# Where polynomials, a last squaring and layer-norm roots stand in a vision transformer's one-core program

## The reference

```python
h = tokens + positions                               # [32, 38, 256]
h = h + attention(layernorm(h))                      # 16 heads of 16, q and k layer-normalized, causal
h1 = h;  z = layernorm(h1)                           # then the FFN's own layernorm with gamma, beta
abel = gelu(xn @ abel_w + abel_b)
logits = xn @ moe_gate_w + moe_gate_b                # 8 experts, top 2, softmax of the two
moe = sum_e w_e * (gelu(xn @ ew1[e] + eb1[e]) @ ew2[e] + eb2[e])
for i in range(3): moe = moe @ expm(gens[i])         # 256 x 256 skew matrices
gate = sigmoid(concat(abel, moe) @ gc_w + gc_b)
out = h1 + residual + abel * (1 - gate) + moe * gate # residual: the FFN's input
```

## Time and profile before

| | |
|---|---|
| three runs | 383.19, 384.49, 385.95 us; median 384.49 |
| the profiled execution | 384.6 us, its span 382.7 us |
| busy, share of the span | TensorE 332.1 us (87%), VectorE 223.6 (58%), ScalarE 175.5 (46%), GpSimd 152.8 (40%) |
| mean granted TensorE clock | 0.955 |
| chain that ended last, by engine | TensorE 71%, VectorE 13%, issue 7%, DMA 4%, ScalarE 2% |
| stages, from the start of the span | attention 75 to 165 us, projection to 188, router and powers to 211, slots to 346, last stage to 380 |

### The profile page before, as it was taken

The page is one execution under the profiler, slowest core; times in us unless marked ns, Lnnn a source line. Parts: engine busy times, 40 slices in busy tenths (PEclk is TensorE's granted clock), DMA queues, the critical chain, the costliest instruction groups (busy, mean ns, idle before and its releaser), DMA issues.

```text
span 382.7 us, 6792 instructions
## 1 busy us (share of the span) xinstructions
PE 332.1 (87%) x2010; PEld 280.3 (73%) x2010; DVE 223.6 (58%) x598; ACT 175.5 (46%) x417; POOL 152.8 (40%) x168
## 2 busy tenths in 40 slices
PE   2999799949999999949989796999999998993895
PEld 1787354539888888836777685999899997892894
DVE  0235459787989999886887287795313231010175
ACT  1000254378898989514433662434344444450231
POOL 1002804050456546361022217588534667852000
PEclk9999899976999999978998999999999999998599
DMA  8742511124111110076404353455324555551442
GB/s 260 269 134 64 200 57 54 55 78 136 48 48 48 46 46 6 2 305 229 143 8 139 97 149 87 149 153 161 115 85 151 167 165 166 178 152 60 144 142 90
DMA packets 20544, 45.78 MB, mean 120 GB/s; under 512 B 2150, under 2 KB 12836, under 8 KB 20260
## 3 DMA queue, kind: packets, MB, share of 16 engines
q1 hardware_dynamic: 17732, 37.80, 30.4%
q0 software_dynamic: 2496, 6.82, 5.3%
q10 hardware_dynamic: 288, 0.81, 0.8%
HBM read 38.20 MB, written 7.22 MB: 119 GB/s over the span
## 4 chain that ended last, share of the span: by engine, by line
PE 71%; DVE 13%; issue 7%; DMA 4%; ACT 2%; POOL 1%; DVEq 1%; POOLq 0%; ACTq 0%; SPq 0%
PE banks L1447 10%; PE banks L1456 9%; PE banks L1389 8%; PE banks L1232 5%; PE banks L1202 5%; PE banks L1309 5%; PE banks L1285 4%; PE banks L1522 3%; PE banks L1327 3%; PE banks L1360 3%; PE banks L1532 3%; PE banks L1272 2%; PE banks L1218 2%; PE banks L1237 2%; PE banks L1258 2%
## 5 line engine op out<-in xcount | busy, mean ns | idle before, releaser
L1447 PE MATMUL banks<-qn_sb,w_sb 128*128 128x128 f32 x416 | 50.9, 275 | 1.0 <-ACT qn_sb L628 1.0
L1456 PE MATMUL banks<-w_sb,sq_sb 128*128 x208 | 49.2, 380 | 0.8 <-DVE pT_sb L1124 0.7
L1447 PEld LDWEIGHTS banks<-qn_sb,w_sb 128*128 128x128 f32 x416 | 48.6, 192 | 1.2 <-ACT qn_sb L628 1.2
L628 ACT ACTIVATE qn_sb<-banks,col_sb 128x128 f32<-128x128 f32 x52 | 21.1, 457 | 56.9 <-PE banks L1434 55.0
L456 POOL DMA_INDIRECT y_rows<-pT_sb,sidx_sb x26 | 25.9, 998 | 45.5 <-DVE pT_sb L1124 43.1
L1456 PEld LDWEIGHTS banks<-w_sb,sq_sb 128*128 128x128 f32 x208 | 38.4, 190 | 6.0 <-issue 1.4
L639 ACT ACTIVATE sq_sb<-banks,col_sb 128x128 f32<-128x128 f32 x104 | 32.4, 369 | 14.8 <-PE banks L1447 13.3
L1124 DVE TENSOR_TENSOR pT_sb<-banks,p_sb 128x256 f32<-128x256 f32 x26 | 11.0, 424 | 47.5 <-PE banks L1456 25.3
L1202 PE MATMUL banks<-wtok_sb,patch_sb 128*114 128x256 f32 x132 | 30.4, 393 | 7.8 <-DMA wtok_sb<-in_w_tok 7.6
L450 POOL DMA_INDIRECT qn_sb<-z_rows,gidx_sb x26 | 28.7, 1103 | 20.1 <-PE banks L1434 13.2
L1202 PEld LDWEIGHTS banks<-wtok_sb,patch_sb 128*114 128x114 f32 x132 | 24.3, 186 | 13.4 <-DMA patch_sb<-in_patches 7.5
(11 more groups left out here) (221 smaller groups left out, 653.2 us busy)
## 6 DMA issues: line engine op xcount, KB each, us to landing
w_sb<-in_w SPq DMA_DIRECT2D x26, 512.0 KB
w_sb<-in_w SPq DMA_DIRECT2D x1, 4096.0 KB, 12.6
patch_sb<-in_patches SPq DMA_DIRECT2D x11, 342.0 KB, 3.1
vrep_sb<-v_rows SPq DMA_DIRECT2D x33, 114.0 KB
qk_sb<-y_rows SPq DMA_DIRECT2D x10, 228.0 KB
v_rows<-v_sb SPq DMA_DIRECT2D x11, 114.0 KB
z_rows<-h_sb SPq DMA_DIRECT2D x11, 114.0 KB
out_rows<-h_sb SPq DMA_DIRECT2D x10, 114.0 KB
```

The costliest lines, as they stand in the source:

```text
L1447: last = nc.tensor.matmul(bank[2 + 2 * s + c // 2][:, (c % 2) * 128:(c % 2 + 1) * 128], w1_sb[:, w0:w0 + 128], xsT_sb[:, (2 * s + k) * 128 ...
L1456: last = nc.tensor.matmul(bank[6 + s][:, 0:D], hidT_sb[:, s * HID + k * 128:s * HID + (k + 1) * 128], w2_sb[:, ds(e * 4 * D + k * D, D)], ...
```

## The change

- `P0_AT` and `P1_AT` go from 2 and 5 to 3 and 6. VectorE runs `poly_first(j)` behind `slot_step(j)` for j = 0, 1, 2, where 0 and 1 stood ahead of slot 0 and 2 behind it.
- Only two of the last three squarings stay in slots 10 and 11. The third matrix is transposed in slot 19 (`LAST_AT`), its product follows behind the last slot. The chain's second product also follows there, in bank 4; its transpose is made in slot 20. `third()` runs behind VectorE's last slot and does two of its steps before the product.
- The roots come in three batches cut at `CUT = (7, 10)`: tiles 0 to 6, whose variances are set in step 8 and whose power stands ahead of `gather_images(9)`; 7 to 9; and 10. `norm_z(0)` and `norm_z(1)` stand ahead of VectorE's `select(10)`, the others are reordered, and `top(t-2)` follows `keep_pre(t)`.
- The ten sizing operations move to the attention's start (`size_generators`), the two scalings to ScalarE, in steps 8 and 9.
- One-column activations on a zero draw the Exp table behind `root(1)`, the Gelu table ahead of the slots, and the Exp table again behind the last Gelu.
- `turn_att(10)`, `output(10)` and `keep_attT(10)` stand one tile later; `rank()` behind the first product, `invert()` behind the seventh.

```diff
@@ -269,8 +269,10 @@
         EARLY = 4
-        P0_AT, P1_AT, MORE_AT, SQ_AT, E_AT = 2, 5, 9, 10, (14, 16)
+        P0_AT, P1_AT, MORE_AT, SQ_AT, E_AT = 3, 6, 9, 10, (14, NS)
         MORE_BANK = (0, 4, 5)
+        LAST_AT = 19
+        CUT = (7, 10)
@@ -428,15 +430,17 @@
             for t in range(NT):
+                if t == NT - 1:
+                    powers(1, 0, CUT[0])
...
                     spread(t + 1)
-            powers(1, 0, 8)
             gather_images(NT - 1)
-            powers(2, 8, NT)
+            powers(2, CUT[0], CUT[1])
+            powers(3, CUT[1], NT)
@@ -524,6 +528,7 @@
             root(1)
+            nc.scalar.activation(al_sb[:, 78:79], con_sb[:, K_ZERO:K_ZERO + 1], ACT.Exp)
@@ -578,6 +583,14 @@
                     keep_attT(t - 1)
+                if isinstance(t, int) and t in (8, 9):
+                    scale_generators(t - 8)
+
+            def scale_generators(n):
+                act.wait_ge(d_gen, 32)
+                act.wait_ge(scale_set, 1)
+                m = (a_sb, aT_sb[:, :])[n]
+                nc.scalar.activation(m, m, ACT.Copy, scale=nrm_sb[:, 12:13]).then_inc(n_scaled, 1)
@@ -597,7 +610,7 @@
             for t in range(NT):
-                if t == 3:
+                if t == 4:
@@ -649,6 +662,11 @@
+            def keep_ET(n, k):
+                act.wait_ge(e_turned, n + 1)
+                nc.scalar.activation(YT[k], bank[0][:, :], ACT.Copy).then_inc(e_evac, 1)
+
+            nc.scalar.activation(al_sb[:, 79:80], con_sb[:, K_ZERO:K_ZERO + 1], ACT.Gelu)
@@ -656,12 +674,14 @@
                 u = j - SQ_AT
-                if 0 <= u < G:
-                    keep_YT(3 * more + u + 1, u % G, 0)
-                if j in E_AT:
-                    n = E_AT.index(j)
-                    act.wait_ge(e_turned, n + 1)
-                    nc.scalar.activation(YT[n], bank[0][:, :], ACT.Copy).then_inc(e_evac, 1)
+                if 0 <= u < 2:
+                    keep_YT(3 * more + u + 1, u, 0)
+                if j == E_AT[0]:
+                    keep_ET(0, 0)
+                if j == LAST_AT:
+                    keep_YT(3 * more + 3, 2, 0)
+                if j == LAST_AT + 1:
+                    keep_ET(1, 1)
@@ -686,6 +706,7 @@
+            nc.scalar.activation(al_sb[:, 77:78], con_sb[:, K_ZERO:K_ZERO + 1], ACT.Exp).then_inc(exp_warm, 1)
@@ -883,11 +904,13 @@
                     norm_k(t + 3, 1 - s)
+                if isinstance(t, int) and t == NT - 1:
+                    norm_z(0)
+                    norm_z(1)
                 select(t, s)
-                if isinstance(t, int) and t == 9:
-                    aggregate(mv2_sb, 0, 8, NT, h1_stats)
-                    variances(0, 8)
-                    scale_generators()
+                if isinstance(t, int) and t == 8:
+                    aggregate(mv2_sb, 0, CUT[0], NT, h1_stats)
+                    variances(0, CUT[0])
@@ -898,8 +921,7 @@
-            def scale_generators():
-                dve.wait_ge(d_gen, 32)
+            def size_generators():
@@ -911,9 +933,13 @@
                 link(nc.vector.tensor_tensor(nrm_sb[:, 11:12], nrm_sb[:, 10:11], nrm_sb[:, 10:11], ALU.subtract))
-                link(nc.vector.tensor_tensor(nrm_sb[:, 12:13], nrm_sb[:, 9:10], nrm_sb[:, 11:12], ALU.add))
-                for m in (a_sb, aT_sb[:, :]):
-                    nc.vector.tensor_scalar(m, m, nrm_sb[:, 12:13], None, ALU.mult).then_inc(n_scaled, 1)
+                nc.vector.tensor_tensor(nrm_sb[:, 12:13], nrm_sb[:, 9:10], nrm_sb[:, 11:12], ALU.add).then_inc(scale_set, 1)
+
+            def norm_z(t):
+                if t in (0,) + CUT:
+                    dve.wait_ge(rstd2, 1 if t == 0 else 2 + CUT.index(t))
+                nc.vector.tensor_scalar(h_sb[0:T, t * D:(t + 1) * D], h1_sb[0:T, t * D:(t + 1) * D], mv2_sb[0:T, 2 * t:2 * t + 1],
+                                        R[1][:, t:t + 1], ALU.subtract, ALU.mult).then_inc(zrow_set, 1)
@@ -921,17 +947,12 @@
             shift(0, 0)
+            size_generators()
...
             idx3 = idx_sb[0:T, :].rearrange("p (t k) -> p t k", k=8)
-
-            def norm_z(t):
-                if t in (0, 8):
-                    dve.wait_ge(rstd2, 1 + t // 8)
-                nc.vector.tensor_scalar(h_sb[0:T, t * D:(t + 1) * D], h1_sb[0:T, t * D:(t + 1) * D], mv2_sb[0:T, 2 * t:2 * t + 1],
-                                        R[1][:, t:t + 1], ALU.subtract, ALU.mult).then_inc(zrow_set, 1)
@@ -945,24 +966,25 @@
-            for t in range(3):
+            for t in range(2, 5):
...
             finish(NT - 2)
-            norm_z(3)
+            aggregate(mv2_sb, CUT[0], CUT[1], NT, h1_stats)
+            variances(*CUT)
             keep_pre(0)
-            norm_z(4)
+            norm_z(5)
             keep_pre(1)
+            norm_z(6)
             finish(NT - 1)
-            aggregate(mv2_sb, 8, NT, NT, h1_stats)
-            variances(8, NT)
+            aggregate(mv2_sb, CUT[1], NT, NT, h1_stats)
+            variances(CUT[1], NT)
             for t in range(2, NT):
-                if t + 3 < NT:
-                    norm_z(t + 3)
                 keep_pre(t)
-                if t >= 4:
-                    top(t - 4)
-            for t in range(NT - 4, NT):
-                top(t)
+                if t + 5 < NT:
+                    norm_z(t + 5)
+                top(t - 2)
+            top(NT - 2)
+            top(NT - 1)
@@ -1133,35 +1155,31 @@
             def third():
+                link(nc.vector.tensor_tensor(Y[0], Y[0], Y[2], ALU.add))
+                for m in range(2):
+                    diagonal = Y[0][:, m * D + m * 128:m * D + m * 128 + 128]
+                    link(nc.vector.tensor_tensor(diagonal, diagonal, eye, ALU.add))
                 dve.wait_ge(e_made, 2)
-                link(nc.vector.tensor_tensor(Y[0], Y[0], Y[2], ALU.add))
                 link(nc.vector.tensor_tensor(yw3[:, :, 0:D], Y[0].rearrange("p (k d) -> p k d", k=2),
-                                             bank[0][:, :].rearrange("p (k d) -> p k d", k=2), ALU.add))
-                for k in range(2):
-                    diagonal = yw3[:, k, k * 128:(k + 1) * 128]
-                    link(nc.vector.tensor_tensor(diagonal, diagonal, eye, ALU.add))
+                                             bank[4][:, :].rearrange("p (k d) -> p k d", k=2), ALU.add))
...
-            poly_first(0)
-            poly_first(1)
...
                 u = j - SQ_AT
-                if 0 <= u < G:
-                    square(3 * more + u + 1, u % G, 0)
+                if 0 <= u < 2:
+                    square(3 * more + u + 1, u, 0)
...
                     second()
-                if j == E_AT[1]:
-                    third()
                 slot_step(j, j % 2, j // 2 if j >= 2 else None)
-                if j == 0:
-                    poly_first(2)
+                if j < G:
+                    poly_first(j)
@@ -1171,7 +1189,9 @@
                             square(3 * i + n + 1, n, MORE_BANK[n])
-
+            square(3 * more + 3, 2, 0)
+            dve.wait_ge(s_kept_cr, 3 * more + G + 3)
+            third()
@@ -1363,14 +1383,14 @@
             for t in range(NT):
-                if t == 3:
-                    turn_att(NT - 1, 0, False)
...
                     output(NT - 2, False)
+                if t == 3:
+                    turn_att(NT - 1, 0, False)
...
                     pre(t - 1, (t - 1) % 2)
-                if t == 3:
+                if t == 4:
@@ -1414,9 +1434,9 @@
                 product(bank[6 + k % 2], AT[n], (A, A2, A3)[k // G][n]).then_inc(x_made, 1)
-                if k == 1:
+                if k == 0:
                     rank()
-                if k == 5:
+                if k == 6:
@@ -1468,14 +1488,17 @@
                                      stop=True).then_inc(counted, 1)
-                if 0 <= u < G:
+                if 0 <= u < 2:
                     pe.wait_ge(s_kept_cr, 3 * more + G + u)
-                    turn_square(bank[0], Y[u % G]).then_inc(s_turned, 1)
-                if j in E_AT:
-                    if j == E_AT[0]:
-                        pe.wait_ge(s_kept_cr, 3 * more + 2 * G)
-                    else:
-                        pe.wait_ge(e_kept, 1)
+                    turn_square(bank[0], Y[u]).then_inc(s_turned, 1)
+                if j == E_AT[0]:
+                    pe.wait_ge(s_kept_cr, 3 * more + G + 2)
+                    turn_square(bank[0], Y[0]).then_inc(e_turned, 1)
+                if j == LAST_AT:
+                    pe.wait_ge(e_kept, 1)
+                    turn_square(bank[0], Y[2]).then_inc(s_turned, 1)
+                if j == LAST_AT + 1:
+                    pe.wait_ge(s_evac, 3 * more + 3)
@@ -1489,13 +1512,12 @@
                     product(bank[0], A4T[n], poly[n]).then_inc(p_made, 1)
-                if 0 <= u < G:
+                if 0 <= u < 2:
                     pe.wait_ge(s_evac, 3 * more + u + 1)
-                    product(bank[0], YT[u % G], Y[u % G]).then_inc(s_made, 1)
```

(13 more changed lines are left out.)

6 lines of the change are left out of this document (3 added, 3 removed).

## The result

The changed kernel takes 370.65 us (median of four runs: 368.37, 368.76, 372.54, 372.73), the kernel before beside it 384.58: a ratio of 0.9632, 95% interval 0.9573 to 0.9692. Its profiled execution took 372.73 us (span 370.9, mean granted clock 0.972), one of the two longer ones; against the 384.6 us of the profile before that is 11.9 us, while the medians are 13.9 apart. I forecast 367.5 us, range 363.5 to 374.5.

The account below looks back on a forecast made before the run. TensorE was busy 87% of the span, with holes at the attention's start and end, the slots' start and before the last stage. 4.4 + 1.8 + 1.7 + 5.8 + 3.4 = 17.1 us; 384.6 - 17.1 = 367.5, range 363.5 to 374.5.

Parts of the forecast that it names:

- Attention's start: Sizing operations and early Exp draw at the attention's start cost and gain nothing: 0, bounds 0 and 1.5 us lost.
- Attention's end: First transpose of normalized rows starts earlier, half clock gone, VectorE newly waits for output(10): gain 4.4 us, bounds 1.5 to 6.5.
- rival (c): output(10) and VectorE's queue hold the attention's end, router's half clock returns: 1.5 instead of 6.2, 372.2 us; chance 0.19.
- Router: Fewer tops, moved rank and inversion, half clock gone in three products, Gelu draw before slots: gain 1.8 us, bounds -1 and 3.5.
- Slots' start: Slot 0's result no longer follows two polynomials, 3.74 us hole goes, slot 4 waits 3.3: gain 1.7 us, bounds 0 and 5.0.
- a longer one kept 1.00: Slot 4's wait: the trace was taken to show full clock after a longer gap, against the skill's warning.
- rival (d): The wait in slot 4 drops the clock, half clock behind it: 369.8 to 370.9 us; chance 0.06.
- Slots' end: Two products leave slots 12 and 16 (3.5 us), third() leaves slot 16 (2.3): gain 5.8 us, bounds 3.5 and 5.9.
- None over 0.5 us behind slot 16: Sign for the late slots: no TensorE wait over 0.5 us behind slot 16.
- Last stage: Moved products shrink TensorE's idleness from 7.6 to 3.3 us, half clock at stage's start goes: gain 3.4 us, bounds -1 and 3.4.
- so I take the whole: Last stage: clock stayed full over a 3.74 us hole, so the whole 3.4 us half-clock loss counts as gained.
- Rival (b): The clock falls over the last wait after all: 1.1 instead of 3.4, 369.8 us, up to 372; chance 0.24.

Follow-up runs that it names:

- f0: The changed kernel again with no edit, beside new runs of the kernel before: 369.67 us, ratio 0.9662.
- g3: The changed kernel without the three early draws of tables on ScalarE: 370.91 us, ratio 0.9635.
- f3: The changed kernel with rank() back behind the second product and invert() behind the sixth: 369.53 us, ratio 0.9644.
- e4: The changed kernel with six more matmuls into an unread bank, keeping TensorE busy before the last stage: 370.58 us, ratio 0.9669.
- f2: The changed kernel with six more matmuls into an unread bank in slot 4, ahead of the wait for poly_second(0): 373.82 us, ratio 0.9742.
- e3: The changed kernel with the attention's end as before (sizing, scaling, roots, normalized rows), rank() and invert() kept at new places: 378.2 us, ratio 0.9886.

## Why the prediction was right, and where not

The forecast, 367.5, is 3.1 us below the median; the direction and most mechanisms held, two on the clock did not, and some of the agreement is luck (below). By its own terms (forecast; in the first profile after; in f0's):

- **Attention's start**, 0: right. TensorE's waits before `turn_q(1)` and `turn_k(1)` are only divided otherwise: 1.94 and 3.44 us before, 3.45 and 1.92 now. From the attention's first transposes to P10 it takes 85.51 us before and 85.47 now, so the sizing, the draw and the first scaling cost nothing; g3 shows it for the draw alone.
- **Attention's end**, 4.4; 4.2; 4.2. The steps held: scalings of 1.57 us (1.5), power 2.65 (2.9), VectorE's wait 2.27 before `finish(10)` (1.8). That the sum is so close is luck, since two sizes were off and cancel: the first transpose came 4.6 us behind P10 where I had 5.3, and from there the last `pre` took 18.05 us where I had 17.1. So that stretch is no shorter than the 17.91 of before although its half clock is gone, and this much of rival (c) came true; its price did not.
- **Router**, 1.8; 2.2; 2.0. The wait before `rank()` is 1.20 us (1.1), and no half clock behind the inversion. But I gave the half clock to the waits that the new places remove; f3 has those waits and no fall, so this 1.9 of the 2.5 us has no shown cause and may be the one execution's. The Gelu load costs nothing, since gather 0's landing comes last there.
- **Slots' start**, 1.7; 0.5; 0.5. Steps and sizes held: hole gone, `poly_second(0)` from 227.3 to 230.4, a wait of 2.61 (3.3). The failed step is the clock behind that wait, of which I wrote "a longer one kept 1.00": rival (d), which I gave 0.06, came true in every profile with this wait, 3.4 us of half clock, so 1.7 us lost. Without it this part would be 2.2, by estimate.
- **Slots' end**, 5.8; 4.0; 5.4. The two products' 3.5 us are sure. The rest depends on gathers: 0.58 us and smaller waits in the first profile, none over 0.25 in f0. "None over 0.5 us behind slot 16" was too strong.
- **Last stage**, 3.4; -0.4; 1.2 (last projection to end: 38.62, 38.98, 37.45). The step that failed, "so I take the whole", failed twice: the clock was not kept, and the clock is not worth that much there. TensorE's idleness shrank as worked out (7.55 to 2.95 us), but the single hole of 3.74 us over which the clock had stayed was the exception: behind idleness of 2.59 us or more it fell in every later case. And 6.8 us at half clock cost TensorE 3.4 us but the stage 1.7 (27.91 against e4's 26.22), because with a fast TensorE the stores' transfers end it. Rival (b) had the mechanism right, and its 1.1 us is f0's figure.
- **Not in the sum**: 1.3 us (f0: 2.5) from the stretch up to P10. Of these 1.3 (f0: 2.0) lie ahead of the attention's first transposes, where nothing is changed; the profile before had half clock from 41.2 to 44.6 us there and those two had none. This is luck of the executions.

So 4.2 + 2.2 + 0.5 + 4.0 - 0.4 + 1.3 = 11.8 us of span for the first profile, 4.2 + 2.0 + 0.5 + 5.4 + 1.2 + 2.5 = 15.8 for f0's (both with rounding; 11.8 and 15.7 measured). Without the start, the change's own gains are 10.5 and 13.3 us of a forecast of 17.1; the larger part of what is missing is the last stage.

The rule I set aside as not agreeing speaks for this result. The Trainium skill, "TensorE: Matmul & The Clock Gate", section HAM oscillation, warns of waits between short bursts of matmuls. The runs agree that such waits drop the clock, in slot 4 and before the last stage, where kept-busy TensorE held 1.00 (f2, e4); but the work ahead of slot 4's wait was no short burst, over 7 us with no wait over 0.25 (220.2 to 227.9 us).

What stays open: why the half clock of the last stage lasts 3.4 us in one execution and 6.8 in another, why the first slot's waits dropped the clock in f2 and e3 alone, what dropped it in the router before, and what makes late gathers later in some executions. Of the attention's end, sizing, power and the order of the rows are not told apart. Stores issued from another queue than the gathers would test the last stage's account; no run has them.

## What to carry to other kernels

Price a hole of idleness with its half clock behind it, even if one row shows a clock that held: one execution's clock is one throw. Before counting regained TensorE speed as time, ask which queue ends the stage; here stores stood behind gathers in SyncE's queue, and 3.4 us of TensorE bought 1.7. Before crediting a change with a half clock that went, look whether it comes and goes where nothing was changed. Work moved into a hole that TensorE has anyway (two products here) is the sure part of such a change.
